# Two places in a Mamba and expert kernel: the inter-chunk products ahead of an expert block, and a state product ahead of a rotation

## The reference

```python
z, x, Bg, Cg, dd_dt, dd_A, trap, angles = split(xn @ W_in)
K = rope(rmsnorm(Bg) + B_bias, theta);  Q = rope(rmsnorm(Cg) + C_bias, theta)
S1 = (Q K^T) * g1 * decay        # inside a chunk of the sequence
S2 = (Q Kprev^T) * g2 * decay
y_intra = S1 @ x + S2 @ xprev
H = chunk_decay * H + Wsum       # the state carried from chunk to chunk
y_inter = (Q * exp(ell)) @ H     # what the earlier chunks give
out = ((y_intra + y_inter + D * x) * silu(z)) @ W_out
```

## Time and profile before

| what | value |
|---|---|
| median of 3 runs | 285.08 us (284.82 to 285.49) |
| profiled execution, its own time | 285.08 us |
| its span, first to last instruction | 283.4 us |
| PE busy | 251.7 us, 89% of the span |
| PEld busy | 219.3 us, 77% |
| DVE busy | 221.5 us, 78% |
| POOL busy | 208.7 us, 74% |
| ACT busy | 149.7 us, 53% |
| mean granted clock of TensorE | 0.963 of full speed |
| moved by DMA | 61.55 MB, mean 217 GB/s |

### The profile page before, as it was taken

How to read it: one execution, slowest core, us unless ns; L and a number is a source line. 1 busy time by engine, 2 the same in 40 slices (tenths; PEclk the granted TensorE clock), 3 DMA queues, 4 the chain that set the end, 5 groups by cost and what they waited for, 6 DMA issues and landing times.

```text
span 283.4 us, 7397 instructions
## 1 busy us (share of the span) xinstructions
PE 251.7 (89%) x2155; PEld 219.3 (77%) x2158; DVE 221.5 (78%) x607; ACT 149.7 (53%) x508; POOL 208.7 (74%) x291
## 2 busy tenths in 40 slices
PE   2999995799999999999999999999999999999600
PEld 0858863688997998899889979997998899889400
DVE  4778998958787969796978778787969796977436
ACT  1765989455456453755363645456453755362033
POOL 8658997858887787888887878787787876665400
PEclk9999999699999999999999999999999999999955
DMA  5630917966978778988888899879878887770095
GB/s 156 220 94 13 325 57 225 319 176 196 260 225 273 247 226 248 264 243 243 237 278 253 222 251 264 243 216 249 288 229 256 262 240 248 238 220 21 23 270 172
DMA packets 68855, 61.55 MB, mean 217 GB/s; under 512 B 6608, under 2 KB 52304, under 8 KB 68816
## 3 DMA queue, kind: packets, MB, share of 16 engines
q1 hardware_dynamic: 66256, 55.83, 65.5%
q0 software_dynamic: 2560, 5.25, 6.7%
HBM read 56.27 MB, written 4.78 MB: 215 GB/s over the span
## 4 chain that ended last, share of the span: by engine, by line
PE 56%; DVE 21%; issue 7%; ACT 5%; DMA 4%; POOL 4%; SPq 1%; DVEq 1%; POOLq 0%; ACTq 0%
PE bank L868 15%; PE bank L911 6%; PE bank L811 5%; PE bank L803 4%; PE bank L863 4%; PE bank L795 4%; PE bank L761 3%; DVE rot L1330 2%; PE bank L766 2%; PE bank L845 2%; DMA decay<-res_dram 2%; DVE sd L1346 2%; PE bank L907 2%; DMA blk<-xn_dram,gidx 2%; DVE rot L1329 1%
## 5 line engine op out<-in xcount | busy, mean ns | idle before, releaser
L868 PE MATMUL bank<-blkT,w_up 128*128 128x128 f32 x512 | 64.7, 281 | 0.4 <-issue 0.4
L868 PEld LDWEIGHTS bank<-blkT,w_up 128*128 128x128 f32 x512 | 62.0, 196 | 2.5 <-issue 2.1
L631 POOL DMA_INDIRECT res_dram<-xrow,sidx x40 | 40.7, 1018 | 22.3 <-DVE xrow L1408 18.0
L577 POOL DMA_INDIRECT blk<-xn_dram,gidx x40 | 42.1, 1053 | 8.6 <-issue 7.4
L911 PE MATMUL bank<-w,xrow 128*128 128x128 f32 x256 | 34.6, 278 | 0.3 <-DVE xrow L1395 0.3
L1086 ACT ACTIVATE xrow<-bank 128x512 f32<-128x512 f32 x40 | 25.2, 629 | 15.7 <-PE bank L868 11.1
L911 PEld LDWEIGHTS bank<-w,xrow 128*128 128x128 f32 x256 | 31.1, 192 | 1.6 <-issue 1.6
L1380 DVE TENSOR_TENSOR xrow<-xrow,bank 128x512 f32<-128x512 f32 x40 | 27.3, 683 | 4.6 <-issue 4.0
L1312 DVE SCALAR_TENSOR_TENSOR kq<-sd,rms,bias_kq 128x512 f32<-128x512 f32 x32 | 23.3, 767 | 8.6 <-POOL rms L588 8.0
L624 POOL TENSOR_TENSOR rstd<-mv,mhalf 128x1 f32<-128x1 f32 x40 | 25.1, 628 | 1.5 <-DVE mv L1392 1.3
L1080 ACT ACTIVATE blkT<-bank 128x128 f32<-128x128 f32 x40 | 12.2, 305 | 21.2 <-PE bank L854 21.2
(11 more groups left out here) (246 smaller groups left out, 625.3 us busy)
## 6 DMA issues: line engine op xcount, KB each, us to landing
w_up<-in_L_ffn_W_dram SPq DMA_DIRECT2D x96, 256.0 KB
w<-in_L_ffn_W_dram SPq DMA_DIRECT2D x48, 256.0 KB
e_row<-e_dram SPq DMA_DIRECT2D x16, 256.0 KB
decay<-l_dram SPq DMA_DIRECT2D x4, 512.0 KB, 5.7
gam<-in_L_ffn_gamma_dram SPq DMA_DIRECT2D x32, 64.0 KB
shift_y<-in_L_ffn_beta_dram SPq DMA_DIRECT2D x32, 64.0 KB
acc<-in_L_attn_u_dram SPq DMA_DIRECT2D x4, 256.0 KB, 3.7
xn_dram<-xrow SPq DMA_DIRECT2D x4, 256.0 KB, 5.1
```

The source lines that it names most:

```text
L577: g.indirect_dma_start(out=blk[:, b % SLOTS, :], out_offset=None, in_=xn_dram, in_offset=bass.IndirectOffsetOnAxis(ap=gidx[:, entry(b):ent ...
L631: g.indirect_dma_start(out=res_dram, in_=res[:, b % HALF, :], in_offset=None, out_offset=bass.IndirectOffsetOnAxis(ap=sidx[:, entry(b):ent ...
L868: last = m(bank[out][:, c * P:(c + 1) * P], w_up[:, u % SETS, n, c * P:(c + 1) * P], blkT[:, b % 2, :], start=True, stop=True)
```

## The change

On PE `inter(t - 1)` stands ahead of `rise(b1)` and `turn_h(b1 - 1)`, and no longer between them and `intra(t - 1)`. On VectorE `fade(t - 1)` stands ahead of `rotate(t)`, and no longer between it and `carry(t - 1)`; it was, and is, called only where both `second` and `first` hold. Nothing else is changed: the helpers and what they wait for are the same.

```diff
@@ -939,11 +939,12 @@
                 if b0 is not None and not ends_ and not begins:
                     down(b0 - 1)
                     turn_block(b0 + 2)
+                if second:
+                    inter(t - 1)
                 if b1 is not None:
                     rise(b1)
                     turn_h(b1 - 1)
                 if second:
-                    inter(t - 1)
                     intra(t - 1)
                 if b1 is not None:
                     down(b1 - 1)
@@ -1449,10 +1450,11 @@
                     diagonal(0)
                 elif first:
                     rot_cosine(t)
+                if second and first:
+                    fade(t - 1)
                 if first and not begins:
                     rotate(t)
                 if second and first:
-                    fade(t - 1)
                     carry(t - 1)
                 if second:
                     gate_y(t - 1)
```

## The result

| | before | after |
|---|---|---|
| median | 284.70 us (12 runs, 284.23 to 285.64) | 286.51 us (12 runs, 285.64 to 287.48) |
| ratio of the times | | 1.0062, 95% interval 1.0045 to 1.0081 |
| profiled execution, its time and span | 285.08, 283.4 us | 285.96, 284.2 us |

The change makes the kernel slower by 0.62% (0.45 to 0.81), 1.8 us. The forecast was 0.9 us more than before and 286.0 us, with 284.3 to 287.8 around it.

A forecast was written before the change was run, and what follows sets the result against it. PE was taken as the bound, busy 26.1 of 26.5 us per cycle. Odd iterations +3.06, t = 9 +0.15, even -2.10 and end -0.20 gave +0.9 on 285.08: 286.0 us, range 284.3 to 287.8.

The forecast's parts named there:

- VectorE's move: VectorE, even iterations: `fade` ahead of `rotate` covers two waits, `gate_y` 0.30 us earlier, L795 0.30 earlier.
- GpSimd's lock: Skill's rule that two-SBUF-input VectorE and SBUF-reading GpSimd instructions exclude each other; would hold `fade` to 164.06, total 289.7 us.
- Rival 3: VectorE's gain does not reach PE, through the GpSimd lock or PE's own changes: +3.2 us, 288.3; chance 0.15.
- TensorE's move: PE: early `inter` adds 0.34 us of shape changes per iteration and uncovers the copy of h; odd iterations 0.51 later.
- rival 1: PE's shape-change drains hide in their new places: -0.5 us, 284.6, no change to be measured; chance 0.20.
- rival 2: Odd iterations at L907: the copy of h stays hidden, sum -3.5 us, 281.6; chance 0.08.
- Loads: SP's weight loads wait for `rise(b1)`, which ends 1 us later; PE never waits for w_up, so nothing was taken.
- the end: Program's last chain, from t = 15 to the final DMA: gains from VectorE's 0.30 earlier, taken as -0.20 us.
- The sum: Whole program: six odd iterations +3.06, t = 9 +0.15, seven even -2.10, end -0.20, together +0.9 us.

The follow-up runs named there:

- VectorE's half alone: Only `fade` moved ahead of `rotate`, TensorE in its old order, against the kernel before: 281.82 us, ratio 0.9899.
- the kernel that gives the cover back: The changed kernel with `turn_h` put between the two halves of the rise: 283.44 us, ratio 0.9946 against the kernel before.
- both halves again: The changed kernel run once more, unchanged, against the kernel before: ratio 1.0056, +1.6 us.
- `state_product` between the halves with VectorE's half: `fade` ahead of `rotate`, and in even iterations PE's `state_product` between `turn_kq`'s transposes of k and q, against the kernel before: 285.45 us, ratio 1.0017.

## Why the prediction was right

The mechanism was right in the loop, the size of the whole was not: a difference of 0.9 us was forecast, and 1.8 and 1.6 were measured. That the time of 286.0 came within 0.5 of the measured 286.51 is in part luck, since I had counted from 285.08, 0.4 above the median of the twelve runs of the kernel before (284.70).

**VectorE's move** was right in each step: `fade` 0.78 after the cosine product (0.77 foreseen), `gate_y` 2.12 (2.13), even iterations 0.31 shorter on the average (0.30). GpSimd's lock did not hold `fade`: it started at 164.44 inside `finish` (164.22 to 164.95) and took 0.41. The Trainium skill (SBUF — State Buffer, Who interferes with whom) would have made it wait; for this pair, whose GpSimd side reads one column, the trace does not agree, and the measurement decides. Rival 3 falls, also in its other form, since L795 did come earlier.

**TensorE's move.** The new shape changes are there, in the change and in a kernel in which one pair of them is the only difference from VectorE's half alone (0.24). L889 is 7.19 behind `project_bc` in place of 6.19, 1.00 later as worked out. The cost agrees with the rule of the Trainium skill (TensorEngine Tiling (Array Packing), Key Properties), and rival 1 falls. L907 is 8.57 behind in place of 7.86, 0.71 later (0.68 foreseen), and the kernel that gives the cover back, and with it 0.41 of the 0.53, shows the reason; rival 2 falls. The odd iteration lost 0.53 to 0.54 (0.51 foreseen), because that delay was 0.03 short. In even iterations PE's extra was hidden with 0.15 to spare (0.14).

**Loads.** The later end of the rise cost nothing: PE has no wait for w_up in any of the profiles.

**The step that failed is the end.** I took 0.20 off there, from VectorE's lead behind t = 15. From `project_bc` of t = 15 to the end of the span are 35.57 us in both traces (and 36.17 in that of both halves again, all of the 0.60 behind the start of the last scatter). The chain after the change shows why:

```profile
258.91 0.44 PE bank L795 x4
259.35 1.79 PE bank L868 x16
261.13 0.91 PE bank L911 x8
262.06 0.31 DVE st L1388
262.85 0.58 POOL rstd L624
...
266.42 2.88 DMA res_dram<-xrow,sidx
```

I had seen that PE's last products would nearly catch up with the stores; they did catch up, and the chain now runs through them. GpSimd's first two stores behind `gate_y` do start earlier, 9.40 and 11.73 behind `project_bc` in place of 9.60 and 11.91, which is the 0.20. Then `finish` (L624) of the last block but one waits for PE's product and starts at 14.19, as before. The last scatter starts 17.76 after `project_bc` of t = 15, as it did before (265.54 less 247.78).

**The sum.** Measured in the loop: 185.87 us before and 187.10 after, from `project_bc` of t = 1 to that of t = 15 (six odd at +0.54, t = 9 +0.18, even ones -2.2 together). That is +1.2 where the forecast had +1.1 for the same part, and with the end +1.2 where it had +0.9. The odd iteration of t = 9 is 15.19 like the others, where the late `carry` had made it 15.01 before, so that it lost only 0.18 (0.15 foreseen).

**What stays open.** The medians lie 1.8 (1.3 to 2.3) and 1.6 (0.9 to 2.2) apart, the loop accounts for 1.2. The two traces compared show +0.8, because the start of the one after the change was 0.35 shorter. That start varies by itself: `project_bc` of t = 1 comes between 60.70 and 63.85 us in the twelve profiles, and the two latest (63.85 and 62.90) are those in which the chain holds the first gather for 7.2 and 7.3 us in place of 4.7. Whether the missing 0.4 to 0.6 us is such a difference in the start, or iterations that are late now and then (one even iteration of 11.88 in place of 11.55 in the trace of both halves again), no run here decides. It is no more than one trace leaves open elsewhere: in the nine other kernels the measured difference from the kernel before lies between 0.8 below and 1.2 above the one that the loops of the two traces show (the largest, `state_product` between the halves with VectorE's half: loop -0.7, measured +0.5).

## What to carry to other kernels

Where an engine is busy for 98% of a loop, read an edit in that engine's list as a move of cover: write down what each moved piece was hiding, here a copy on another engine between a transpose and its use, and who hides it now. Count the changes of array shape on each side of the moved piece; a neighbour of the same shape was worth 0.24 to 0.34 us. And try the halves of a change apart: one of these was worth -1.0%, the other +1.3%, and together they looked like a small loss of 0.6%. Don't expect them to add up: a lead that one engine gains is worth something only where the other still waits for it.

## What the runs showed of the hardware that I had not expected

A pair of shape changes is not one price: around a single transpose it cost 0.25 us, around a rise of 16 instructions 0.34, with 0.20 of it at the change from 128 x 64 back to 128 x 128. An instruction with two SBUF inputs on VectorE took 0.85 us beside GpSimd's `square_own` (512 elements wide), but its usual 0.41 beside the root of one column. And 0.46 us of idle time stood ahead of one `carry`, that of t = 9, in all three profiles with VectorE's old order, and in none of the nine with the new. The profile names no releaser for it in one of the three and VectorE's own `fade` in the others; its cause is open.
